# A ring of four PSUM banks that also takes the attention outputs, a new order of work, and identity products on TensorE in the first element

## The chip, the cores and the metric

The kernel runs on one core of one Trainium2 chip. Its engines are called as the profile calls them: PE (matrix products), ACT (activations and copies), DVE (vector work), POOL (small vector work), SP (issues the DMAs). Each engine runs its own queue of instructions in order and waits on semaphores for the others. The metric is the device time of one launch in microseconds. The kernel before took 1795.92 us (median of 3 runs, 1793.83 to 1796.07).

## What is computed

The input x is 32 elements (a batch) of 128 tokens by 256 channels, with a context of the same shape. Four layers follow each other, all in fp32:

```python
x = L0(x, ctx)      # x + attention of element 0 only: one 128x256 block, added to all 32 elements
x = L1(x, ctx)      # RMS norm -> in_proj -> convolution of 4 taps -> silu -> state space scan
                    # -> gate -> RMS norm -> out_proj, residual; then cross attention, 8 heads, padding mask
x = L2(x, ctx)      # causal self attention (16 heads), norm; cross attention, norm; two 256x256 layers, norm
x = L3(x, ctx)      # causal cross attention (16 heads), norm; 256 -> 1024, gelu, 1024 -> 256
```

The scan of L1 is computed in its quadratic form: 128x128 matrices of decays and of pair products (C times B), and then products with the inputs. So an element needs four attentions (numbered 1 to 4 here; attention 0 is L0's and runs once).

## The kernel before, in words

Each of the 32 elements goes through the same 80 or so named tasks: `xhatT` (transpose of the normalised input), `K1`, `V1`, `z0`, `z1`, `xbc0`, `xbc1` (projections), `conv0`, `conv1`, `silu` (DVE and ACT), `pairs` (PE: the pair product `CB`, then a transpose `xh`), `ld` (PE: sums of log decays), `decayed` (DVE), `Y` (PE: the scan's output), `uT`, `proj`, `xnT`, `Q1`, then for each attention `quads` (scores), `scores` (maxima on DVE, exponentials on ACT), `turn` (transposes of the exponentials on PE, copied out by ACT), `values` (products with V), `back` (transpose of the output), `finish` and `norm` (DVE, with a power on POOL in between), and at the end `up0`, `up1`, `down`. On POOL, `dt` and `softplus` are some 20 tiny steps that end in the step sizes, `am` writes the 128x1024 matrix `decay` from them (L1483), and `z0` stands for the gating of z (L1476 and L1477).

The work of several elements is interleaved: while one element is in its last layer, five younger ones are in earlier ones. The order is written out by numbers. `TASKS` gives each task a place in a period of 14 units, element n adds 14 n, `FIRST` and `LAST` shift the tasks of the first eight and last six elements, `SETUP` places what is done once, and `SHIFT` moves a task on ACT, DVE, POOL or SP against its place on PE. Every engine then executes its share of the tasks in the sorted order. Nothing reorders them at run time, so an instruction that waits holds up everything behind it on its engine.

PSUM has eight banks of 128x512 floats. Before, three of them form the ring (`bank[0..2]`), four hold scores, and one is `output`, for `values` alone. A job of the ring is one PE task that fills one bank: job k takes bank k mod 3, in the order of PE's queue. `claim` makes PE wait until job k-3 has been read (semaphore `bank_read`), and the reader, ACT or DVE, waits for `bank_full`. `values` waits for `output_read` instead, and signals by four semaphores `att_full0..3`, one for each 32 rows.

The lines that the text speaks of: L614 transposes (`flip`), L620 and L626 projections, L676 scores, L708 and L718 `values`, L788 `CB`, L795 `ld`, L805 `Y` on PE; L1026 the exponential inside softplus, L992 exponentials of the scores on ACT; L1268 the convolution's steps, L1274 silu's last step, L1282 to L1284 softplus' quotient, L1170 the second half of a norm on DVE.

Of the kernel before, what the change touches and what calls it, by code (L numbers as in the profile page):

```python
# [54 lines left out]
    Q3=37.543, V3=40.148, e3=38.349, n3=39.865, finish3=40.144, norm3=42.354, x4T=42.781, fc1=43.499, fc2=44.959, norm4=44.907,
    K4=45.195, V4=46.057, x5T=46.08, Q4=47.009, finish4=59.44, norm5=59.058, x6T=54.763, up0=56.224, up1=56.439, down=81.976,
    store=80.382, quads1=22.371, scores1_0=22.334, turn1_0=23.905, values1=25.647, quads2=29.409, scores2_0=29.402,
    scores2_1=30.19, turn2_0=31.6, turn2_1=31.809, values2=33.339, attT2=32.223, back2=34.871, quads3=38.411, scores3_0=38.673,
    scores3_1=39.48, turn3_0=40.43, turn3_1=40.496, values3=40.816, attT3=37.17, back3=41.465, quads4=47.824, scores4_0=48.781,
    scores4_1=49.099, turn4_0=50.021, turn4_1=50.308, values4=52.319, attT4=49.603, back4=54.003)  # L60

FIRST = dict(
    loadx=(-1.5564, -2.6165, 0.0017, 3.3707, -0.1049, -5.3785, 0.0062, -0.1984),
    loadc=(-1.6132, 0.0057, 5.0634, 0.2142, -0.0297, -0.0279, 0.0007, -1.9086),
    x1=(-1.6224, 0.0057, -0.0189, -3.0408, -0.0182, -0.03, 0.0203, 0.0012),
    x1r=(-0.0087, -0.0139, 0.0017, -0.0293, 0.0014, 0.001, 0.0251, 0.4294),
    xhat=(0.6085, 0.1762, -0.4078, 0.0017, 0.0014, 0.001, 0.0007, 0.0012),
# [1529 lines left out]
```

## Time and profile before

| | |
|---|---|
| median of 3 runs | 1795.92 us |
| the profiled execution | 1793.13 us, of which the span of instructions 1791.1 us |
| PE busy | 1684.8 us (94% of the span) |
| ACT busy / DVE busy / POOL busy | 1368.2 (76%) / 1345.6 (75%) / 549.9 (31%) |
| mean granted PE clock | 0.978 of full |
| chain that ended last | PE 78%, DVE 14%, ACT 3%, issue 3%, POOL 2% |

Engines are busy side by side, so the shares don't add up. A group of PE rows such as `L620 ... x8` counts passes: an fp32 product of 128 columns is two passes. The time of a group's last pass is modelled and overlaps the next group; the distance from one start to the next is what PE really took. A bracket such as `[0.42 <-DVE conv L1274]` is idle time ahead of the group and who ended it. The loading of the weights fills the DMA engines in the first 50 us; afterwards they move 10 GB/s.

### The profile page before, as it was taken

How to read it: one execution, taken by the hardware profiler on the slowest of the kernel's cores; microseconds unless marked ns; L12 is line 12 of the kernel's file. 1: busy time of each engine (PE TensorE's matmuls, PEld its weight loads, DVE VectorE, ACT ScalarE, POOL GpSimd, SP SyncE). 2: the span in 40 equal slices, each digit the busy share in tenths (PEclk: the TensorE clock that was granted, in tenths of full speed). 3: DMA queues.
4: the chain of work that ended last, by engine and by line, in shares of the span. 5: the costliest groups of instructions: out<-in, count | busy, mean ns of one | idle time of the engine just before them, and what ended most of it. 6: DMA issues, size and time to landing. Idle time of an engine off the chain costs nothing.

```text
span 1791.1 us, 54559 instructions
## 1 busy us (share of the span) xinstructions
PE 1684.8 (94%) x21072; PEld 1437.7 (80%) x21072; DVE 1345.6 (75%) x3355; ACT 1368.2 (76%) x4026; POOL 549.9 (31%) x1288
## 2 busy tenths in 40 slices
PE   5679999999999999999999999999999999999876
PEld 4467888888888888888888888888888888888765
DVE  3477788877777888778788877778888778878542
ACT  2267887887888788788878877887888788778763
POOL 1233233332333333233333333323333233333110
PEclk7799999999999999999999999999999999999988
DMA  7000000000000000000000000000000000000000
GB/s 257 7 7 8 8 2 11 11 11 11 11 2 11 11 11 11 11 11 2 11 11 11 11 11 11 2 11 11 11 11 10 11 2 11 11 8 5 5 4 9
DMA packets 26174, 26.89 MB, mean 15 GB/s; under 512 B 2240, under 2 KB 25024, under 8 KB 25792
## 3 DMA queue, kind: packets, MB, share of 16 engines
q1 hardware_dynamic: 25920, 23.41, 4.0%
q8 instruction: 171, 2.80, 0.7%
q14 instruction: 83, 0.68, 0.1%
HBM read 19.21 MB, written 4.19 MB: 13 GB/s over the span
## 4 chain that ended last, share of the span: by engine, by line
PE 78%; DVE 14%; ACT 3%; issue 3%; POOL 2%; DVEq 0%; DMA 0%; SPq 0%; POOLq 0%; ACTq 0%
PE ring L626 21%; PE ring L620 20%; PE ring L614 17%; PE output L718 5%; PE score L676 5%; DVE conv L1274 4%; PE ring L795 3%; PE ring L805 2%; ACT exps L992 2%; PE output L708 2%; POOL stat L1437 1%; DVE tz L1312 1%; DVE res L1170 1%; DVE bn L1157 1%; DVE res L1358 1%
## 5 line engine op out<-in xcount | busy, mean ns | idle before, releaser
L992 ACT ACTIVATE exps<-score,neg_max 128x128 f32<-128x128 f32 x1808 | 495.0, 412 | 73.3 <-DVE neg_max L1181 70.5
L1181 DVE TENSOR_REDUCE neg_max<-score 128x4 f32<-128x512 f32 x452 | 286.4, 681 | 76.5 <-PE score L676 74.4
L1437 POOL TENSOR_TENSOR stat<-stat 128x1 f32<-128x1 f32 x224 | 129.3, 577 | 530.7 <-DVE stat L1153 529.8
L998 ACT COPY weights<-ring 128x512 f32<-128x512 f32 x452 | 244.0, 604 | 57.2 <-PE ring L614 55.5
L614 PE MATMUL ring<-const,exps 128*128 128x128 f32 x1808 | 248.7, 279 | 24.2 <-ACT exps L992 10.4
L614 PEld LDWEIGHTS ring<-const,exps 128*128 128x128 f32 x1808 | 198.4, 142 | 60.1 <-issue 27.7
L1268 DVE SCALAR_TENSOR_TENSOR conv<-raw,vectors,conv 128x128 f32<-128x128 f32 x576 | 168.4, 348 | 6.8
L620 PE MATMUL ring<-actT,w_q 128*128 128x128 f32 x1024 | 142.5, 282 | 0.5 <-ACT actT L964 0.5
L620 PEld LDWEIGHTS ring<-actT,w_q 128*128 128x128 f32 x1024 | 127.3, 192 | 10.9 <-issue 6.3
L964 ACT COPY actT<-ring 128x256 f32<-128x256 f32 x224 | 81.9, 378 | 70.7 <-PE ring L614 70.6
L676 PE MATMUL score<-K,QB 32*128 32x128 f32 x3616 | 134.9, 283 | 0.1
L676 PEld LDWEIGHTS score<-K,QB 32*128 32x128 f32 x3616 | 113.8, 188 | 16.4 <-issue 15.3
L620 PE MATMUL ring<-actT,w_up 128*128 128x128 f32 x1024 | 123.2, 280 | 0.5 <-ACT actT L964 0.5
L620 PEld LDWEIGHTS ring<-actT,w_up 128*128 128x128 f32 x1024 | 120.5, 197 | 0.9 <-ACT actT L964 0.9
L626 PE MATMUL ring<-w_down,gT 128*128 128x256 f32 x512 | 118.0, 384 | 0.0
L1004 ACT COPY attT<-output 128x512 f32<-128x512 f32 x97 | 56.8, 585 | 75.0 <-PE output L718 75.0
L718 PE MATMUL output<-weights,V 128*32 128x128 f32 x3104 | 106.6, 279 | 2.4 <-issue 1.5
L626 PEld LDWEIGHTS ring<-w_down,gT 128*128 128x128 f32 x512 | 94.9, 190 | 14.8
L620 PE MATMUL ring<-cT,w_k 128*128 128x128 f32 x768 | 104.1, 280 | 0.0
L626 PE MATMUL ring<-w_v,cT 128*128 128x256 f32 x384 | 99.2, 381 | 2.4 <-ACT tz L1040 2.4
L1499 POOL TENSOR_TENSOR V<-V,keep 128x256 f32<-128x256 f32 x64 | 39.7, 621 | 200.2 <-DVE keep L1351 112.1
L620 PEld LDWEIGHTS ring<-cT,w_k 128*128 128x128 f32 x768 | 98.5, 196 | 1.7
(163 smaller groups left out, 3531.2 us busy)
## 6 DMA issues: line engine op xcount, KB each, us to landing
cT<-in_ctxT SPq DMA_DIRECT2D x32, 128.0 KB, 2.2
x_in<-in_x SPq DMA_DIRECT2D x32, 128.0 KB, 2.1
out<-result SPq DMA_DIRECT2D x32, 128.0 KB, 1.7
row_all<-in_rows SPq DMA_DIRECT2D x1, 1420.0 KB, 10.0
w_in<-in_in_proj SPq DMA_DIRECT2D x1, 1288.0 KB, 7.3
w_k<-in_k SPq DMA_DIRECT2D x4, 256.0 KB, 5.8
w_v<-in_v SPq DMA_DIRECT2D x4, 256.0 KB, 5.9
w_q<-in_q SPq DMA_DIRECT2D x4, 256.0 KB, 6.5
```

Source lines behind the costliest of these rows:

```text
L614: last = nc.tensor.transpose(t[:, c * P:(c + 1) * P], src[:, c * P:(c + 1) * P], ident)
L620: last = mm(t[:, at:at + P], w[:, c, cols:cols + P], xT[:, c, :], start=(c == 0), stop=(c == n - 1))
L626: last = mm(t[:, at:at + hi - lo], xT[:, c, :], w[:, c, lo:hi], start=(c == 0), stop=(c == n - 1))
L676: last = mm(score[:, r, at:at + P], QB[rows_of, l, c, e, :], keys[rows_of, l, c, :], start=(not masked and at == 0), stop=(at + P == width))
L718: last = mm(output[ROWS_OF[r], four * P:(four + 1) * P], V2[:, l, h, :], exps_of(t, heads_of(a_, t).index(h)), start=True, stop=True)
L964: nc.scalar.copy(dst.rearrange("p c k -> p (c k)"), t[:, 0:n]).then_inc(read, 1)
L992: last = run(exps[:, n, h * P:(h + 1) * P], of, ACT.Exp, bias=neg_max[:, m, h:h + 1])
L998: nc.scalar.copy(weights[:, buffer(it, a_, l, t, WEIGHT_BUFFERS), half * 4 * P:(half + 1) * 4 * P], t_[:, :]).then_inc(read, 1)
L1181: nc.vector.tensor_reduce(neg_max[:, m, 4 * half:4 * half + 4].rearrange("p (b h) -> p b h", b=each), score[:, first:first + each, 0:4 // ...
L1268: last = stt(conv[:, l % 2, c, :], raw[:, l % 2, c, k:k + P], conv_w[:, c, k:k + 1], conv[:, l % 2, c, :], ALU.mult, ALU.add)
L1274: stt(conv[:, l % 2, :, :], raw[:, l % 2, :, TAPS - 1:], 1.0, conv[:, l % 2, :, :], ALU.add, ALU.mult).then_inc(S["xbc"], 1)
L1437: tt(stat[:, l, 10:11], stat[:, l, 2:3], stat[:, l, 4:5], ALU.pow).then_inc(S[done], 1)
```

## The change

Three things change together.

1. `output` is gone and the ring has four banks. `values1` to `values4` (and `values0`) are jobs of the ring like the others; their readers (`attT` on ACT, `finish1` on DVE) wait for `bank_full` in place of `att_full3` and release `bank_read` in place of `output_read`. What waited for `output_read` on PE (`back`, `Wo`) now waits for the `values` job's bank to be read, unless its own bank makes it wait for the same thing.
2. All tables of the order have new numbers: PE, ACT, DVE, POOL and SP execute the same tasks in another order, in the steady part as in the first and last elements.
3. `SPARE`: ahead of eleven tasks of the first element (one is of the second) PE executes 80 products in all of the 128x128 identity with itself, into the first 128 columns of the bank that the task is about to fill. Nothing reads them.

```diff
 TASKS = dict(
-    loadx=-19.632, loadc=-0.373, x1=-12.582, x1r=18.202, xhat=40.805, xhatT=6.043, dt=11.125, softplus=10.471, am=-3.466,
...
+    loadx=-39.297, loadc=-21.957, x1=-31.388, x1r=0.609, xhat=34.036, xhatT=-8.817, dt=1.27, softplus=-2.884, am=-12.308,
...
-RING_BANKS = 3
+RING_BANKS = 4
...
+SPARE = {("turn0_0", 0): 5, ("turn0_1", 0): 4, ("bias", 0): 7, ("xhatT", 0): 17, ("pairs", 0): 18, ("Y", 0): 5, ("uT", 0): 4,
+         ("turn1_0", 0): 5, ("Wo", 0): 6, ("Y", 1): 4, ("x4T", 0): 5}
...
-NO_RING += [f"{task}{a_}" for task in ("quads", "values", "attT") for a_ in PARTS]
+NO_RING += [f"{task}{a_}" for task in ("quads", "attT") for a_ in PARTS]
...
-        output = pb("output", [P, 512])
...
+            def spare(it, what, lane, times):
+
+                t, full = claim(it, what, lane)
+                for _ in range(times):
+                    mm(t[:, 0:P], ident, ident, start=True, stop=True)
...
             def values(it, a_, l):
 
-                if a_:
-                    pe.wait_ge(S["output_read"], nth_output(it, a_, l) - 1)
+                output, full = claim(it, f"values{a_}", l)
...
-                            last.then_inc(S[f"att_full{r}"], 1)
+                            last.then_inc(full if r == TILES - 1 else S[f"att_full{r}"], 1)
 
             def back(it, a_, l):
-                pe.wait_ge(S["output_read"], nth_output(it, a_, l))
+                evacuated(it, f"values{a_}", l, back_job(a_, l))
...
             def program():
                 for task, l, i in ORDER["PE"]:
+                    if i == 0 and (task, l) in SPARE:
+                        spare(Of(i), RING_JOBS.get(task, task).split()[0], l, SPARE[task, l])
                     if task in do:
...
             def out_turned(it, a_, l):
-                for r in range(TILES):
+                for r in range(TILES - 1):
                     act.wait_ge(S[f"att_full{r}"], nth_output(it, a_, l))
-                nc.scalar.copy(attT[:, att_buffer(it, a_, l), :], output[:, :]).then_inc(S["output_read"], 1)
+                t, read = filled(it, f"values{a_}", l)
+                nc.scalar.copy(attT[:, att_buffer(it, a_, l), :], t[:, :]).then_inc(read, 1)
...
                 def finish1(l):
-                    for r in range(TILES):
+                    for r in range(TILES - 1):
                         dve.wait_ge(S[f"att_full{r}"], nth_output(it, 1, l))
-                    step(nc.vector.reciprocal(rec1[:, :], output[:, D:]))
+                    t, read = filled(it, "values1", l)
+                    step(nc.vector.reciprocal(rec1[:, :], t[:, D:]))
```

**PE, the first element.** From the transpose of attention 0's output (`attT`) to the sums of log decays (`decay,const`). Before:

```order
L614 MATMUL ring0<-const,attT 128x128 x4
L614 MATMUL ring1<-const,att 128x128 x2
L620 MATMUL ring2<-cT,w_k1 128x128 x4
L626 MATMUL ring0<-w_in,actT 128x264 x2
L620 MATMUL ring1<-actT,w_in 128x128 x6
L620 MATMUL ring2<-actT,w_in 128x128 x6
L626 MATMUL ring0<-w_v1,cT 128x256 x2
L626 MATMUL ring1<-w_in,actT 128x256 x2
L788 MATMUL ring2<-conv 128x128
L614 MATMUL ring0<-const,conv 128x128 x4
L795 MATMUL ring1<-decay,const 128x512
L795 MATMUL ring2<-decay,const 128x512
```

In the changed kernel (`ring3<-const 128x128 x17` are identity products):

```order
L569 MATMUL ring2<-const,attT 128x128 x4
L576 MATMUL ring3<-const 128x128 x17
L569 MATMUL ring3<-const,att 128x128 x2
L581 MATMUL ring0<-cT,w_k1 128x128 x4
L581 MATMUL ring1<-actT,w_in 128x128 x6
L581 MATMUL ring2<-actT,w_in 128x128 x6
L587 MATMUL ring3<-w_in,actT 128x264 x2
L587 MATMUL ring0<-w_v1,cT 128x256 x2
L587 MATMUL ring1<-w_in,actT 128x256 x2
L576 MATMUL ring2<-const 128x128 x18
L748 MATMUL ring2<-conv 128x128
L569 MATMUL ring3<-const,conv 128x128 x4
```

The two halves of `xbc` (`actT,w_in ... x6`) now come ahead of `z1` (`w_in,actT 128x264`), and 17 and 18 identity products stand ahead of `xhatT` and of the pair product of `conv`.

**POOL, the middle of the program**, around `am` (`decay<-const,dts`) and the gating of z (`tz<-tz`, `zs<-tz,zs`). Before:

```order
L1490 TENSOR_TENSOR q_first<-QB,const 128x16
L1482 TENSOR_TENSOR dts<-dts,row_all 128x8
L1483 TENSOR_TENSOR decay<-const,dts 128x1024
L1509 TENSOR_TENSOR fc1T<-res,row_all 128x256
L1476 TENSOR_SCALAR tz<-tz 128x512
L1477 TENSOR_TENSOR zs<-tz,zs 128x512
```

And now:

```order
L1445 TENSOR_TENSOR dts<-dts,row_all 128x8
L1446 TENSOR_TENSOR decay<-const,dts 128x1024
L1462 TENSOR_TENSOR V<-V,keep 128x16x16
L1464 COPY V<-keep 128x16
L1400 TENSOR_TENSOR stat<-stat 128x1
L1472 TENSOR_TENSOR fc1T<-res,row_all 128x256
L1400 TENSOR_TENSOR stat<-stat 128x1
L1453 TENSOR_TENSOR q_first<-QB,const 128x16
L1439 TENSOR_SCALAR tz<-tz 128x512
L1440 TENSOR_TENSOR zs<-tz,zs 128x512
```

`decay` was written right ahead of the gating of z. It now comes ahead of a masking of V (`V<-V,keep`) and of two powers (`stat<-stat`), and right ahead of the gating stand only a power and `q_first`.

**DVE, the middle of the program**, around silu's last step (`conv<-raw,conv`). Before:

```order
L1358 SCALAR_TENSOR_TENSOR res<-att,mask,res 128x256
L1157 BN_STATS bn<-res 128x6
L1158 BN_AGGR stat<-bn 128x2
L1153 TENSOR_SCALAR stat<-stat 128x1
L1168 SCALAR_TENSOR_TENSOR att<-res,stat,row_all 128x256
L1170 SCALAR_TENSOR_TENSOR res<-att,stat,row_all 128x256
L1274 SCALAR_TENSOR_TENSOR conv<-raw,conv 128x768
L1347 TENSOR_SCALAR nonzero<-ring 128x16
L1181 TENSOR_REDUCE neg_max<-score 128x4 x2
```

And now:

```order
L1321 SCALAR_TENSOR_TENSOR res<-att,mask,res 128x256
L1120 BN_STATS bn<-res 128x6
L1121 BN_AGGR stat<-bn 128x2
L1116 TENSOR_SCALAR stat<-stat 128x1
L1164 TENSOR_TENSOR res<-x_in,att 128x256
L1131 SCALAR_TENSOR_TENSOR att<-res,stat,row_all 128x256
L1133 SCALAR_TENSOR_TENSOR res<-att,stat,row_all 128x256
L1116 TENSOR_SCALAR stat<-stat 128x1
L1310 TENSOR_SCALAR nonzero<-ring 128x16
L1237 SCALAR_TENSOR_TENSOR conv<-raw,conv 128x768
L1144 TENSOR_REDUCE neg_max<-score 128x4 x2
```

Silu's last step now comes after `x1` (`res<-x_in,att`), its mean square (the last `stat<-stat`) and `e2` (`nonzero<-ring`), which stood behind it.

## Rows read from the trace of the kernel before

**Rows 1.** Busy us of each engine (x instructions) by stretch, clock, DMA share, GB/s.
```profile
30.40:66.20 35.80, 20.23 (x135) 15.15 (x135) 15.57 (x44) 7.21 (x19) 11.95 (x28) 0.69 0.14 47
...
92.90:139.40 46.50, 36.54 (x472) 29.57 (x472) 34.22 (x85) 28.29 (x85) 16.22 (x37) 0.95 0.02 7
...
919.10:1648.00 728.90, 717.77 (x9171) 616.43 (x9171) 585.02 (x1457) 593.45 (x1751) 240.20 (x561) 1.00 0.03 9
...
1740.00:1791.10 51.10, 35.50 (x249) 29.47 (x247) 12.28 (x30) 17.73 (x50) 3.40 (x6) 0.81 0.03 8
```

**Rows 2.** PE in time order: start, us, line, op, tiles; idle before and releaser.
```profile
919.07 0.49 PE L788 MATMUL ring<-conv 128*128 128x128 f32 x2 [0.42 <-DVE conv L1274]
...
920.73 2.15 PE L795 MATMUL ring<-decay,const 128*128 128x512 f32 x4
922.71 1.03 PE L626 MATMUL ring<-w_fc,fc1T 128*128 128x256 f32 x4
```

**Rows 3.** The same view of PE, 14 elements later.
```profile
1647.98 0.49 PE L788 MATMUL ring<-conv 128*128 128x128 f32 x2 [0.42 <-DVE conv L1274]
```

**Rows 4.** Waits of PE from 200 to 1600 us: total, times, longest.
```profile
PE ring L788 <- DVE conv L1274: 11.0, 26, 0.4
```

**Rows 5.** POOL and DVE in time order where the element 17 pair product waits.
```profile
916.25 1.95 POOL L1483 TENSOR_TENSOR decay<-const,dts 128x1024 f32<-128x1024 f32 x1
916.37 2.65 DVE L1274 SCALAR_TENSOR_TENSOR conv<-raw,conv 128x768 f32<-128x768 f32 x1
...
919.57 1.51 POOL L1476 TENSOR_SCALAR tz<-tz 128x512 f32<-128x512 f32 x1
```

**Rows 6.** The same for element 3, from 184 us.
```profile
188.71 0.95 DVE L1274 SCALAR_TENSOR_TENSOR conv<-raw,conv 128x768 f32<-128x768 f32 x1
...
188.93 2.49 POOL L1483 TENSOR_TENSOR decay<-const,dts 128x1024 f32<-128x1024 f32 x1
...
190.92 0.49 PE L788 MATMUL ring<-conv 128*128 128x128 f32 x2
```

**Rows 7.** L1274 alone: ns at least, median and most.
```profile
L1274 DVE SCALAR_TENSOR_TENSOR conv<-raw,conv x32: 950/2646/2648, 45.7 to 1645.3; 128x768 f32<-128x768 f32 x32
```

**Rows 8.** PE in time order, the first element.
```profile
30.43 0.69 PE L614 MATMUL ring<-const,att 128*128 128x128 f32 x2 [3.85 <-DVE att L1209]
...
46.68 0.79 PE L788 MATMUL ring<-conv 128*128 128x128 f32 x2 [7.08 <-DVE conv L1274]
...
49.70 3.50 PE L795 MATMUL ring<-decay,const 128*128 128x512 f32 x4 [1.37 <-POOL decay L1483]
...
60.03 3.44 PE L626 MATMUL ring<-w_out,tz 128*128 128x256 f32 x8 [0.72 <-issue]
...
66.17 0.48 PE L614 MATMUL ring<-const,att 128*128 128x128 f32 x2 [2.48 <-DVE att L1163]
...
92.89 0.49 PE L788 MATMUL ring<-conv 128*128 128x128 f32 x2 [1.08 <-DVE conv L1274]
```

**Rows 9.** PE in time order, 125 to 200 us.
```profile
135.81 0.69 PE L614 MATMUL ring<-const,res 128*128 128x128 f32 x2 [3.65 <-DVE res L1170]
...
142.04 1.88 PE L795 MATMUL ring<-decay,const 128*128 128x512 f32 x4
143.76 1.03 PE L626 MATMUL ring<-w_fc,fc1T 128*128 128x256 f32 x4
...
152.43 1.89 PE L626 MATMUL ring<-w_out,tz 128*128 128x256 f32 x8
```

**Rows 10.** ACT in time order, the first element's exponential of its step sizes.
```profile
39.05 0.20 ACT L1026 ACTIVATE dts<-dts 128x8 f32<-128x8 f32 x1
```

**Rows 11.** PE in time order, the last element.
```profile
1754.25 3.62 PE L626 MATMUL ring<-w_down,gT 128*128 128x256 f32 x16
...
1766.92 1.93 PE L718 MATMUL output<-weights,V 128*32 128x128 f32 x32 [0.83 <-issue]
...
1775.49 5.93 PE L620 MATMUL ring<-actT,w_up 128*128 128x128 f32 x32 [0.46 <-ACT actT L964]
```

More of the change, by code:

```diff
@@ L55 @@
[L55 to L58, printed above, removed]
@@ new lines @@
+    loadx=-39.297, loadc=-21.957, x1=-31.388, x1r=0.609, xhat=34.036, xhatT=-8.817, dt=1.27, softplus=-2.884, am=-12.308,
+    xbc0=-7.003, xbc1=-5.859, z1=-5.461, z0=1.147, K1=-7.656, V1=-0.645, conv0=10.153, conv1=1.914, silu=8.942, pairs=2.154,
+    ld=3.18, decayed=4.453, Y=4.486, uT=5.016, proj=5.731, xnT=7.896, Q1=8.272, finish1=10.278, Wo=13.01, x2T=13.36, K2=15.065,
+    Q2=13.819, V2=18.506, e2=15.211, n2=15.74, finish2=23.561, norm2=19.381, x3T=23.838, row=23.91, K3=24.14, Q3=25.27, V3=24.234,
@@ new lines @@
+    e3=26.002, n3=26.41, finish3=21.372, norm3=36.468, x4T=29.166, fc1=31.148, fc2=31.994, norm4=36.026, K4=31.657, V4=32.925,
+    x5T=32.94, Q4=33.558, finish4=46.075, norm5=40.873, x6T=41.8, up0=42.154, up1=42.297, down=68.294, store=78.752, quads1=9.708,
+    scores1_0=10.704, turn1_0=11.473, values1=12.06, quads2=15.325, scores2_0=16.842, scores2_1=17.864, turn2_0=18.34,
+    turn2_1=18.516, values2=19.823, attT2=22.328, back2=21.152, quads3=25.921, scores3_0=25.992, scores3_1=26.33, turn3_0=26.863,
@@ L602, in evacuated, with evacuated_all @@
                     pe.wait_ge(bank_read[b], use + 1)
-            def evacuated_all(it, *jobs):
+            def evacuated_all(it, *jobs, then=None):
                 last = {job(it, *j)[0]: j for j in sorted(jobs, key=lambda j: place(it, *j))}
                 for j in last.values():
-                    evacuated(it, *j)
+                    evacuated(it, *j, then)
             def flip(it, what, lane, src, n):
@@ L699, in exps_of @@
                     return weights[:, buffer(it, a_, l, t, WEIGHT_BUFFERS), i * P:(i + 1) * P]
-                evacuated_all(it, *V_job, *[j for t in range(PARTS[a_]) for j in turn_jobs(a_, l, t)])
+                evacuated_all(it, *V_job, *[j for t in range(PARTS[a_]) for j in turn_jobs(a_, l, t)], then=(f"values{a_}", l))
                 if a_ == 1:
@@ L720, in values @@
                         if four == H16 // TILES - 1:
[L721 removed]
+                            last.then_inc(full if r == TILES - 1 else S[f"att_full{r}"], 1)
             def back(it, a_, l):
[L724 removed]
+                evacuated(it, f"values{a_}", l, back_job(a_, l))
                 flip(it, *back_job(a_, l), attT[:, att_buffer(it, a_, l), :], 4)
@@ L828, in Wo @@
             def Wo(it, l):
-                pe.wait_ge(S["output_read"], nth_output(it, 1, l))
+                evacuated(it, "values1", l, ("Wo", l))
                 project(it, "Wo", l, square["o1"], actT[:, l])
```

245 lines of the change are left out of this document (96 added, 149 removed).

## The prediction

> **What bounds the kernel now.** First the busy time by stretch [rows 1]: from 919 to 1648 us, which is 14 elements, PE is busy 717.77 of 728.9 us, so the middle of the program is PE's and the other engines can only hurt by making it wait. In the first element (30 to 66 us) PE is busy 20.2 of 35.8 us at a granted clock of 0.69, from 93 to 139 us it idles 10 of 46.5 us, and in the last 51 us it idles 15.6. I then looked for the period: `CB` of an element starts at 919.07 and 14 elements later at 1647.98 [rows 2, 3], so an element costs 728.91 / 14 = 52.06 us.
>
> How much of that is work? Eight fp32 products of 128 columns take from 142.04 to 143.76, 0.215 us each [rows 9]. Adding up the start-to-start times of all of an element's PE tasks where nothing waits gives me 50.7 us. So 1.36 us of each period are lost: 0.80 as visible idle time (11.13 / 14, rows 1), the rest inside groups. The idle time has one large author: `CB` waits 0.42 us for silu's last step on DVE, 26 times between 200 and 1600 us [rows 4]. Inside a group, `ld` takes from 920.73 to 922.71, 1.98 us, where 1.72 do [rows 2, 9], for its halves need banks that others still read. What is left, some 0.6 us, are hand-overs of 0.2 to 0.3 us in which a transpose or a `turn` claims one of three banks or waits for a norm.
>
> Why silu is late is in the DVE rows: L1274 takes 0.95 us at least and 2.65 as a rule [rows 7]. In the rule it starts 0.12 us after POOL began to write `decay`, and ends 0.82 us after POOL is done [rows 5]: it did nothing until POOL had finished. In element 3 silu started 0.22 us ahead; it took 0.95, POOL took 2.49, and `CB` did not wait [rows 6]. Whoever is first makes the other wait.
>
> **Part 1, the ring.** 58 jobs an element on three banks become 62 on four. Measured in PE work between the end of a bank's last job and its next claim, by my count along both orders, the shortest distances were 0.49 us (`Q4` after `x5T`) and a dozen of 0.88; now they are 0.94 (`turn3`'s second half after `down`), 1.32, and then 1.6 to 1.8. A copy of a bank takes 0.4 to 0.6 us and starts 0.2 after PE, so distances of 0.88 are where the hand-overs bite. The new risk is that `values1` holds a ring bank through DVE's reciprocal: the bank is wanted by `turn3` four jobs later, 4.0 us of PE work on, and I count 3.4 us until `finish1` is done. No instruction is added outside SPARE. Value: between 0 and the 0.6 us of hand-overs; I take 0.35 an element, since the norm waits among them only shrink.
>
> **Part 2, the middle's order.** `decay` leaves silu's neighbourhood on POOL, which removes 1.7 us from DVE's path to `CB`. What is late next? I followed the ACT queue from `up0`: gelus, tanh, gelus, the copy of `K2`, the square of `x1`, then z0's two copies, which release the gating (1.5 us on POOL, rows 5). Silu stands behind `x1`'s mean square and `e2`. By durations of the trace silu starts some 0.3 us ahead of the gating and ends 0.1 to 0.2 us after PE reaches `CB`. So of the 0.42 I keep 0.2. With `pairs` no longer pushed, `ld` loses its 0.26 (its claims now lie 1.6 us and more from the last use). Further `x2T` and `x4T` stood 0 to 0.9 us of work behind the products they depend on and now have 1.8 and 5.3 us. In sum 0.35 (ring) + 0.22 (`CB`) + 0.25 (`ld`) = 0.8 us an element, bounds 0 and 1.2, over the 29 elements from the third on: 23 us (0 to 35).
>
> **Part 3, the start.** Three things. (a) The clock. `ld` takes 3.50 us in element 0 and 1.88 later, `proj` 3.44 and 1.89 [rows 8, 9]: half rate. Each came behind idle time. At the full rate the pieces on the first element's chain (outputs' product, transposes, projections of `z` and `xbc`, `ld`, `uT`, `proj`) are some 7 us shorter. (b) The order. The two `xbc` now directly follow `K1`, so the convolution begins 1.8 us earlier in PE work; the exponential of the step sizes, at 39.05 us behind V1 in ACT's queue [rows 10], now comes right after `z1`, so that POOL's chain to `decay` can start some 3 us earlier; and ahead of `xnT` PE executes `K1` and half of `xbc` of element 1 (2.2 us), where it idled 2.48 us at 66.17 [rows 8]. Together with (a) I get `xnT` at about 58 us, with 2.2 us more work done: 10 us gained. In element 1, `conv0` moves ahead of `finish1`, and `CB`, at 92.89 us after a wait of 1.08 [rows 8], comes at about 79. (c) From there to `CB` of element 2 the largest idle time is 3.65 us before `x4T` [rows 9], of which `K2` and `z0` (1.8 us), now in between, take half; but other waits of this stretch [rows 1] stay. I carry 15 us for the start as a whole and 2 for the ramp behind it.
>
> The price are 80 products. At 0.215 us they are 17 us, at half rate 34. The waits they stand in were 3.85 us before `xhatT` and 7.08 before `CB` [rows 8]; 17 and 18 products at the full rate fill 3.7 and 3.9 of them. `CB`'s wait shrinks by the work under (b) to about 6 us, so 18 fit at full rate and not at half rate. The seven before `bias` (1.5 us) push `back` by some 0.8 us, but `values` ahead of them is 0.9 shorter if the clock is up. So at the full rate I price SPARE at nothing, at half rate up to 17 us minus the remaining slack, some 8.
>
> **Part 4, the end.** `down` of element 29 stood between `Q4` and `quads4` of the last element, where ACT needs 1.8 us to copy `Q4` [rows 11]. It now stands between `values4` and `back4`, where only 0.9 us are covered: `quads4` starts 1.8 us earlier and `back4` 2.7 later than it could. `values4` and `up0` ran at a lower rate there (1.93 and 5.93 us, rows 11), and `down` may too. I take 1 us lost, bounds -3 and +4.
>
> **The sum**, against the profiled execution: 1791.1 - 23 - 15 - 2 + 1 = 1752 us of span, and 2.0 us around it, 1754. The median stands 2.8 us above that execution (1795.92 to 1793.13), so the forecast is 1757 us.
>
> **Rivals.** (A) The start as forecast, the middle unchanged: the 1.36 us are then set by DVE and ACT (80 to 81% busy each, rows 1), and a wait removed at `CB` returns a task later, as the 0.72 us of idle time in front of other tasks would. For it: both have only 10 us of 52 to spare, and their queues are as rigid as PE's. Against it: half of PE's idle time has one author [rows 4], and its cause is seen. 1796 - 16 = 1780 us.
>
> (B) The identity products cost what they bring: the granted clock doesn't stay up between them, and they are served at half rate, 34 us, half of it outside the waits. The start gains 5 instead of 17: 1769 us.
>
> (C), the slower side: the gating of z wins against silu. Then silu waits the whole L1476 (1.5 us) and takes its 0.95 afterwards, and `CB` waits some 2.0 us in each element in place of 0.42. It decides from the point where z0's copies end less than about 0.25 us after `e2`'s read; my margin is 0.3. The middle then loses 1.6 and keeps the other 0.6 of gain: 29 x 1.0 = 29 us slower, the start 16 faster: 1796 + 13 = 1809 us.
>
> In a sentence of the Trainium skill (SBUF — State Buffer, "Who interferes with whom"): a DVE instruction with two SBUF inputs contends with a GpSimd instruction that reads SBUF, through an exclusive lock held for the whole instruction. The trace agrees (2.65 and 0.95 us, rows 5 to 7). The page speaks for both the gain of part 2 and rival C, as the gating reads SBUF too; by it the price of C is a whole L1476.
>
> **How the numbers follow.** Forecast 0.60, A 0.14, B 0.12, C 0.10, and 0.04 for something that I don't see, half of it slower. The forecast's own range is 1742 to 1772; A adds the part up to 1782, and with B below it 0.8 is held by 1740 to 1785. This kernel's runs lie within 0.13%, so 0.2% tells a change. Faster: forecast, A, B and half of the rest, 0.88, less 0.04 in which A and B are both true and next to nothing is left, which is the same; slower: C and half of the rest, 0.12.
>
> **What would show it.** In the profile after: L1274 at a median near 0.95 us and `CB` waiting under 0.2 us (part 2), or L1274 at 2.4 and `CB` waiting 2 us (C). Starts of `CB` 51.2 us apart in the middle (forecast), 52 (A). `ld` of element 0 at about 1.9 us and the clock of 30 to 60 us above 0.9 (a), or below 0.8 with the identity products at 0.43 us each (B). `CB` of element 1 near 79 us. In the last 51 us, `back4` 2 to 3 us after `values4`. Wrong altogether would be a period longer than 52.1 us with L1274 short: then a new wait has taken the place of the old ones.

## The result and the profile after

The changed kernel takes 1737.63 us (median of 4 runs, 1736.11 to 1740.05), the kernel before 1795.41 in the same runs: a ratio of 0.968, interval 0.966 to 0.970. The forecast was 1757 us with 1740 as the low end. The sign was right, the size was not: the change gains 57.8 us where 39 were forecast. The span of the profiled execution fell from 1791.1 to 1734.3 us, by 56.8. One execution of each of two kernels below (5762 us of i1, its profiled one, and 3523 us of i3) was disturbed and is left out of their times, so i1 has no row in the table.

First the stretches that answer to [rows 1], in the same columns (length; busy us of PE, of its weight loads, of DVE, ACT and POOL; clock, DMA share, GB/s):

```profile
30.00:66.00 36.00, 27.43 (x221) 23.40 (x222) 16.35 (x47) 8.36 (x23) 12.81 (x29) 0.86 0.15 52
88.80:132.00 43.20, 37.66 (x494) 31.57 (x491) 31.64 (x83) 28.02 (x84) 15.05 (x37) 0.98 0.02 5
891.70:1598.70 707.00, 704.59 (x9170) 611.37 (x9171) 570.31 (x1454) 588.09 (x1748) 230.72 (x561) 1.00 0.03 9
1683.20:1734.30 51.10, 35.45 (x272) 29.28 (x260) 12.20 (x32) 19.82 (x53) 3.43 (x6) 0.87 0.03 9
```

The third row is the middle, the same 14 elements and 9170 products as before. PE idles 2.4 us there where it idled 11.1. But its busy time fell as well, from 717.77 to 704.59 us for the same work: the larger part of the gain (13.2 of 21.9 us) never was idle time.

PE in time order, middle of the program (start, us, line, tiles, count, idle before and its releaser), answers to [rows 2, 3]:

```profile
891.73 0.49 PE L748 MATMUL ring<-conv 128*128 128x128 f32 x2 [0.19 <-DVE conv L1237]
...
893.38 1.88 PE L755 MATMUL ring<-decay,const 128*128 128x512 f32 x4
895.11 1.05 PE L581 MATMUL ring<-cT,w_k 128*128 128x128 f32 x8
...
942.26 0.49 PE L748 MATMUL ring<-conv 128*128 128x128 f32 x2 [0.19 <-DVE conv L1237]
```

In this element `CB` waits 0.19 us instead of 0.42, as forecast (0.2), and `ld` takes from 893.38 to 895.11, 1.73 us instead of 1.98, as forecast. `CB` starts 14 elements after 891.73 at 1598.71: 706.98 / 14 = 50.50 us an element. That is below the 50.7 us that the prediction took for pure work.

The waits of PE from 200 to 1600 us (total, times, longest), where [rows 4] had 11.0 us in its first row:

```profile
PE ring L748 <- DVE conv L1237: 4.1, 21, 0.2
PE ring L569 <- ACT attT L967: 1.7, 1, 1.7
PE ring L569 <- DVE res L1133: 1.5, 2, 1.3
```

Silu against the gating of z, POOL and DVE in time order, answers to [rows 5]:

```profile
890.25 1.51 POOL L1439 TENSOR_SCALAR tz<-tz 128x512 f32<-128x512 f32 x1 [1.43 <-ACT tz L1003]
890.32 1.36 DVE L1237 SCALAR_TENSOR_TENSOR conv<-raw,conv 128x768 f32<-128x768 f32 x1
```

And silu's line alone, all 32 (ns at least, median and most), answers to [rows 7]:

```profile
L1237 DVE SCALAR_TENSOR_TENSOR conv<-raw,conv x32: 947/1351/1365, 46.0 to 1597.6; 128x768 f32<-128x768 f32 x32
```

The gating starts 0.07 us ahead of silu: the condition of rival C has come true. But silu then takes 1.36 us, not 1.5 + 0.95. It loses 0.41, and is not held until POOL has ended at 891.76: it ends at 891.68.

The first element, PE in time order, answers to [rows 8]:

```profile
31.96 0.44 PE L569 MATMUL ring<-const,att 128*128 128x128 f32 x2 [2.04 <-DVE att L1172]
...
40.05 4.18 PE L576 MATMUL ring<-const 128*128 128x128 f32 x36
47.03 0.80 PE L748 MATMUL ring<-conv 128*128 128x128 f32 x2 [2.79 <-DVE conv L1237]
49.77 3.73 PE L755 MATMUL ring<-decay,const 128*128 128x512 f32 x4 [1.09 <-POOL decay L1446]
...
64.60 0.44 PE L569 MATMUL ring<-const,att 128*128 128x128 f32 x2 [0.47 <-DVE att L1126]
```

`CB` of element 0 comes at 47.03 us (46.68 before), `xnT` at 64.60 where 58 were forecast, `CB` of element 1 at 88.83 where 79 were. The 18 identity products ahead of `CB` run at nearly the full rate (36 passes in 4.18 us, 0.23 us a product). But 2.79 us of idle time are left behind them, and `ld` is served at half rate again: 3.73 us. The clock from 30 to 60 us is 0.83, where the forecast asked for above 0.9 and rival B for below 0.8.

The last element, answers to [rows 11]:

```profile
1709.92 1.08 PE L678 MATMUL ring<-weights,V 128*32 128x128 f32 x32 [0.96 <-ACT weights L960]
1710.93 3.72 PE L587 MATMUL ring<-w_down,gT 128*128 128x256 f32 x16
...
1718.61 0.44 PE L569 MATMUL ring<-const,res 128*128 128x128 f32 x2 [3.52 <-DVE res L1133]
1719.51 5.21 PE L581 MATMUL ring<-actT,w_up 128*128 128x128 f32 x32 [0.46 <-ACT actT L926]
```

From `values4` to the end it is 24.4 us (24.2 before). `back4` (not shown, at 1714.49 us) starts 4.6 us after `values4` and not 2 to 3. The end gained, but ahead of this row.

**Where the 56.8 us are.** The starts of `CB` cut the span of any of these kernels in three: up to `CB` of element 2, the 29 elements to `CB` of element 31, and what lies behind. This table has every version whose trace could be read so; ratios are against the kernel before in the same runs, with their 95% intervals. The last three columns come from one profiled execution each, which is not always a typical one: that of g1 took 5.2 us more than g1's median, that of f4 2.9 us less.

| version | us | ratio | CB of 2 | per element | behind CB of 31 |
|---|---|---|---|---|---|
| before | 1795.4 | | 139.4 | 52.02 | 143.1 |
| after | 1737.6 | 0.968 (.966-.970) | 132.0 | 50.58 | 135.6 |
| f1 ring of four alone | 1771.4 | 0.987 (.986-.989) | 144.1 | 51.23 | 142.0 |
| f2 new order, three banks | 1827.0 | 1.018 (1.016-1.019) | 136.6 | 53.39 | 140.5 |
| f3 after without SPARE | 1739.8 | 0.969 (.968-.971) | 135.9 | 50.57 | 136.1 |
| f4 before with SPARE | 1790.2 | 0.997 (.996-.999) | 133.4 | 52.07 | 142.0 |
| g1 `decay` back at the gating | 1740.1 | 0.970 (.969-.971) | 132.2 | 50.74 | 139.7 |
| g2 silu first | 1731.9 | 0.965 (.964-.966) | 130.8 | 50.41 | 136.2 |
| g3 earlier preparation | 1737.9 | 0.968 (.967-.969) | 131.7 | 50.65 | 135.7 |
| g4 `down` back | 1737.0 | 0.968 (.966-.969) | 131.3 | 50.60 | 136.7 |
| h1 before, `decay` early | 1818.9 | 1.014 (1.012-1.015) | 143.8 | 52.77 | 141.7 |
| h2 f1, `decay` early | 1792.4 | 0.999 (.998-1.000) | 143.2 | 52.03 | 141.3 |
| h3 g2 and g3 | 1733.0 | 0.966 (.964-.967) | 132.0 | 50.46 | 138.2 |
| h4 f1 with three banks | 1926.9 | 1.073 (1.071-1.075) | 144.6 | 56.74 | 143.1 |
| i2 g2, products at the end | 1731.2 | 0.965 (.963-.966) | 131.2 | 50.46 | 136.8 |
| i3 h3, products at both ends | 1729.6 | 0.964 (.962-.965) | 127.1 | 50.44 | 135.5 |
| i4 after, V1 moved back | 1780.3 | 0.992 (.991-.993) | 134.5 | 52.01 | 136.4 |

So the start gives 7.4 us, the middle 29 x 1.445 = 41.9, the end 7.5. The prediction had 17, 23 and -1.

### The profile page after: what moved, and what is told of

It is laid out like the page before. It is cut to its first block, busy times and chain, and to the rows that moved or that the text cites. A ratio compares the mean times of both kernels' runs of the same rounds, so it can differ in the third digit from the quotient of the medians.

```text
span 1734.3 us, 54906 instructions
## 1 busy us (share of the span) xinstructions
PE 1664.1 (96%) x21232; PEld 1438.0 (83%) x21232; DVE 1313.4 (76%) x3355; ACT 1357.1 (78%) x4026; POOL 533.5 (31%) x1288
## 4 chain that ended last, share of the span: by engine, by line
PE 88%; DVE 7%; issue 2%; ACT 1%; POOL 1%; DMA 0%; DVEq 0%; SPq 0%; POOLq 0%; ACTq 0%
PE ring L581 26%; PE ring L587 22%; PE ring L569 18%; PE score L637 6%; PE ring L678 5%; PE ring L755 3%; PE ring L765 2%; DVE conv L1237 2%; PE ring L668 2%; PE ring L816 1%; DVE conv L1231 1%; PE score L628 1%; DVE neg_max L1144 1%; PE ring L748 1%; ACT exps L954 1%
## 5 line engine op out<-in xcount | busy, mean ns | idle before, releaser
L960 ACT COPY weights<-ring 128x512 f32<-128x512 f32 x452 | 257.3, 658 | 44.0 <-PE ring L569 42.3
L569 PE MATMUL ring<-const,exps 128*128 128x128 f32 x1808 | 240.1, 275 | 11.6 <-ACT exps L954 7.9
L569 PEld LDWEIGHTS ring<-const,exps 128*128 128x128 f32 x1808 | 210.2, 142 | 33.9 <-ACT exps L954 15.8
L581 PE MATMUL ring<-actT,w_q 128*128 128x128 f32 x1024 | 138.0, 278 | 2.5 <-ACT actT L926 2.5
L637 PEld LDWEIGHTS score<-K,QB 32*128 32x128 f32 x3616 | 113.8, 188 | 21.9 <-issue 21.7
L926 ACT COPY actT<-ring 128x256 f32<-128x256 f32 x224 | 86.4, 386 | 56.3 <-PE ring L569 56.3
L678 PE MATMUL ring<-weights,V 128*32 128x128 f32 x3104 | 104.9, 276 | 4.1 <-issue 2.1
L967 ACT COPY attT<-ring 128x512 f32<-128x512 f32 x97 | 57.0, 588 | 63.9 <-PE ring L678 63.3
L678 PEld LDWEIGHTS ring<-weights,V 128*32 128x32 f32 x3104 | 79.0, 109 | 25.7 <-issue 25.5
```

Of the source, the lines that this page charges most:

```text
L569: last = nc.tensor.transpose(t[:, c * P:(c + 1) * P], src[:, c * P:(c + 1) * P], ident)
L581: last = mm(t[:, at:at + P], w[:, c, cols:cols + P], xT[:, c, :], start=(c == 0), stop=(c == n - 1))
L637: last = mm(score[:, r, at:at + P], QB[rows_of, l, c, e, :], keys[rows_of, l, c, :], start=(not masked and at == 0), stop=(at + P == width))
L678: last = mm(output[ROWS_OF[r], four * P:(four + 1) * P], V2[:, l, h, :], exps_of(t, heads_of(a_, t).index(h)), start=True, stop=True)
L926: nc.scalar.copy(dst.rearrange("p c k -> p (c k)"), t[:, 0:n]).then_inc(read, 1)
L960: nc.scalar.copy(weights[:, buffer(it, a_, l, t, WEIGHT_BUFFERS), half * 4 * P:(half + 1) * 4 * P], t_[:, :]).then_inc(read, 1)
```

## The experiments

**f1 and f2: the two halves of the change.** f1 has the code after (four banks, the outputs of attention in them) with the tables of numbers before and no identity products. f2 is the reverse: the code before with the tables after.

```
f1:  RING_BANKS = 4      TASKS, FIRST, LAST, SETUP, SHIFT: before   SPARE = {}
f2:  RING_BANKS = 3, output in its own bank                         tables: after
```

> The ring of four banks with the outputs in it, in the order of before, without identity products. Theory R (the fourth bank carries the middle of the program): the period falls from 52.0 to about 51 us and the time to about 1765 us. Theory O (the order carries it): CB still waits 0.42 us and L1274 still takes 2.65 us, only hand-overs of banks get shorter, 0.3 us an element: about 1786 us.

> The new order with the three banks and the separate output bank of before, without identity products. Theory O: the period is 50.9 us or less and the time about 1755 us, nearly all of the gain of the middle. Theory R, and a theory B by which each needs the other: the new order was made for four banks, with three its shortest distances are short again, the period stays at 51.5 us or more and the time at 1775 us or more.

The ring alone takes 0.80 us off an element. The order alone makes it 1.37 us longer, but on four banks it takes another 0.65 off. The gain is not a sum of two: the new order is written for four banks. The waits of PE in f2 show what three banks do to it; all the releasers are copies and reads that empty a bank:

```profile
PE ring L572 <- DVE keep L1303: 20.5, 26, 0.8
PE ring L578 <- ACT weights L950: 12.5, 26, 0.5
PE ring L572 <- ACT raw L983: 11.1, 26, 0.8
PE ring L572 <- ACT V L933: 9.4, 26, 0.7
PE ring L566 <- DVE result L1341: 7.1, 25, 0.3
```

In f1 `CB` still waits its 0.42 us, 26 times, but `ld` falls to 1.74 and the wait of a `turn` on `tz` is gone but for one:

```profile
912.17 0.49 PE L795 MATMUL ring<-conv 128*128 128x128 f32 x2 [0.42 <-DVE conv L1284]
...
913.83 1.88 PE L802 MATMUL ring<-decay,const 128*128 128x512 f32 x4
915.57 1.13 PE L634 MATMUL ring<-w_fc,fc1T 128*128 128x256 f32 x4
```

So the ring alone gives `ld`'s 0.25 us, which the prediction booked to the order. The order alone gives it as well: in f2, with three banks, `ld` starts at 942.54 and the next group at 944.26 us (1.72). Either half is enough, and the 0.25 must not be counted twice.

**h4: is it the fourth bank, or the outputs in the ring?** f1 with one number changed, so that the outputs of attention share three banks.

```
-RING_BANKS = 4
+RING_BANKS = 3
```

> The code of the changed kernel in the order of before, without identity products, with a ring of three banks that also takes the outputs: the bank that was freed is left unused. Theory R2 (what gives the 24 us of the ring alone is the fourth bank): 62 jobs then share three banks, values has to wait for banks and holds them through its readers, and the time is 1805 us or more. Rival (what gives it is that the outputs rotate, so that values no longer waits for output_read): 1790 us or less.

```profile
PE ring L634 <- DVE keep L1361: 63.9, 23, 3.7
PE ring L795 <- DVE conv L1284: 10.1, 24, 0.4
```

An element takes 4.7 us more than before, 5.5 more than with four. A job waits up to 3.7 us for a bank that DVE is to read. Part of the 5.5 us is the clock, which falls with these waits: over the 14 elements behind `CB` of element 17 it is granted 0.96 in h4 and 1.00 in f1, and PE is busy 748.2 us there against 709.8. Sharing costs; the bank pays for it and for 0.8 us more.

**g1 and g2: silu against POOL.** g1 puts `decay` back beside the gating on POOL. g2 puts silu earlier into DVE's queue, ahead of `x1r` and `e2`.

```
g1:  FIRST am=(0, 0, ...)           SHIFT POOL am=10.06185 -> 15.59
g2:  SHIFT DVE silu=-6.49255 -> -6.84255
```

> The changed kernel with one task moved on POOL: the writing of decay (am) again right ahead of the gating of z, as before the change. Theory L (what made silu late before was POOL reading SBUF at the same time, and the 128x1024 write of decay costs it 1.7 us, while the gating costs it 0.4): L1237 goes from 1.36 back to 2.6 us or more, CB waits 1.2 us or more, the period goes from 50.5 to 51.5 to 52.5 and the time to 1765 to 1795 us. Rival (the moves on DVE and ACT ended the wait, POOL's place is of no weight): L1237 stays under 1.4 and the time within 2 us.

> The changed kernel with silu's last step moved ahead of x1's mean square and e2 on DVE, some 0.9 us earlier than the gating of z on POOL. Theory L: it takes 0.95 us in place of 1.36, CB no longer waits 0.19 us, the period falls from 50.53 to 50.2 to 50.35, the time to 1728 to 1733 us. Rival (0.2 us come back at the next task of PE): period and time stay within 2 us of the changed kernel.

POOL and DVE of g1 in time order:

```profile
894.58 1.96 POOL L1446 TENSOR_TENSOR decay<-const,dts 128x1024 f32<-128x1024 f32 x1
...
895.88 1.47 DVE L1237 SCALAR_TENSOR_TENSOR conv<-raw,conv 128x768 f32<-128x768 f32 x1
```

Silu starts 1.30 us into the write of `decay`, ends 0.81 us after it, and `CB` waits 0.31. Yet from element 17 to 31 an element takes 50.45 us, after's 50.50. DVE gets back elsewhere more than it loses at silu (1.47 against 1.36 us): its step `res<-att,res` (L1319), which runs into the write of `decay` in the order after (0.67 us at the median, 200 to 1600 us), takes 0.42 in g1. g1's profiled execution is longer where its clock was lower: 5.5 us from `CB` of element 2 to that of 17 (0.993 against 0.998) and 4.1 behind the last `CB` (0.889 against 0.924). The medians differ by 2.4 us and the intervals of the ratios overlap. So `decay`'s place beside the gating is not what the order gains by, and the expected cost did not show. DVE and POOL of g2:

```profile
886.05 0.95 DVE L1237 SCALAR_TENSOR_TENSOR conv<-raw,conv 128x768 f32<-128x768 f32 x1
...
887.17 1.51 POOL L1439 TENSOR_SCALAR tz<-tz 128x512 f32<-128x512 f32 x1 [1.43 <-ACT tz L1003]
```

Silu is done before the gating begins, takes 0.95 us, and `CB` waits in no element but the first: another 0.17 us an element, 1731.9 us in all. Here the rest of `CB`'s wait (0.19) is worth what it was.

**h1 and h2: `decay` moved early, with nothing else.** In the kernel before (h1) and in f1 (h2) `decay` is written right behind the step sizes, as in the new order.

```
h1, h2:  SHIFT POOL am=16.54316 -> 14.4761; FIRST and LAST of am: those of softplus
```

> The kernel before with one task moved: on POOL the writing of decay directly follows the step sizes, some 10 us ahead of silu's last step, as in the changed kernel. Theory L (silu is late in it only because it waits for this write): L1274 takes 0.95 us, CB doesn't wait 0.42 us, the period falls from 52.02 to 51.4 to 51.6 us and the time by 12 to 18 us, to about 1780. Rival (with three banks the next hand-over takes the time): CB's wait goes, the time falls by under 5 us.

> The ring of four banks in the order of before, without identity products (1771.4 us, period 51.25), with the same one move on POOL. Theory L: CB no longer waits, the period falls to about 50.8 and the time to 1756 to 1760 us; what then still separates it from the changed kernel without identity products (1739.8 us) is the rest of the new order. Rival: the wait returns elsewhere and the time stays above 1766 us.

The theory that silu's lock was the order's gain falls here. In the middle `CB` waits no more in either, and both are slower than without the move, by 0.75 us an element (h1) and 0.80 (h2). The waits of PE in h1 say where:

```profile
PE ring L614 <- DVE res L1170: 17.0, 27, 0.9
PE ring L614 <- DVE res L1337: 13.3, 25, 1.5
```

The 0.42 us at `CB` have become 0.6 and 0.5 us in front of two transposes of a residual. DVE and POOL of h1 in time order say why:

```profile
920.50 1.90 POOL L1483 TENSOR_TENSOR decay<-const,dts 128x1024 f32<-128x1024 f32 x1
921.68 0.99 DVE L1356 TENSOR_TENSOR res<-att,res 128x256 f32<-128x256 f32 x1
...
931.98 1.05 DVE L1170 SCALAR_TENSOR_TENSOR res<-att,stat,row_all 128x256 f32<-128x256 f32 x1 [0.51 <-POOL stat L1437]
932.04 0.72 POOL L1509 TENSOR_TENSOR fc1T<-res,row_all 128x256 f32<-128x256 f32 x1
```

The write of `decay` left silu and met another DVE step, L1356, which takes 0.99 us at the median here and in h2 and 0.42 in the kernel before and in f1. POOL's `fc1T`, which stood behind `decay`, moved up and met a norm, L1170: it takes over 0.9 us once an element in h1 and h2, and once in all from 200 to 1600 us in the kernel before. Both DVE steps end 0.27 us after POOL's, and each delays one of the two transposes. It looks like rival A's "a wait removed at `CB` returns a task later", but what returns is the same interference at two other steps. In the order after, the first of these steps takes 0.67 us and no norm is lengthened (L1133: 0.49 us at most from 200 to 1600 us).

**i4: how much is distance in PE's queue worth?** One number of the new table: V1, a product of 0.87 us that stands between `Wo` and `x2T`, goes back behind `K3`.

```
-V1=-0.645
+V1=-3.83
```

> The changed kernel with one number of the table changed: V1 goes back to where the kernel before had it, between K3 and V3 of the other stage, so that it no longer stands between the output projection and x2T; the PE work between them falls from 1.78 to 0.89 us. Theory distance: a hand-over of 0.89 us costs 0.2 to 0.3 us each time, 5 to 10 us in all: 1742 to 1748 us, with a new wait of L569 on DVE's res (L1133) in each element. Rival: distance does not matter as long as silu is in time; within 2 us of 1737.6.

It costs 42.7 us, 1.46 an element: as much as the whole change gained in the middle. Four to nine times what was expected. The waits of PE:

```profile
PE ring L569 <- ACT V L943: 9.6, 26, 0.4
PE ring L569 <- DVE res L1133: 6.9, 26, 0.4
PE ring L569 <- DVE res L1300: 5.8, 22, 0.3
PE ring L678 <- issue: 5.5, 26, 0.5
```

The second and third are one thing. DVE's timeline of the kernel after begins this stretch with the reciprocal of attention 1 and ends it with the norm that `xhatT` waits for:

```profile
925.30 1.75 DVE L1295 RECIPROCAL rec<-ring 128x256 f32<-128x256 f32 x1
...
939.27 0.48 DVE L1133 SCALAR_TENSOR_TENSOR res<-att,stat,row_all 128x256 f32<-128x256 f32 x1
939.92 0.15 DVE L1116 TENSOR_SCALAR stat<-stat 128x1 f32<-128x1 f32 x1 [0.17 <-ACT att L971]
```

Between these rows DVE has no idle time: 14.4 us of queue from 925.30 on. In i4 it is the same (950.30 to 964.85). Over these 15 us DVE's queue is at least as long as PE's work, though PE is 99.7% busy over the middle as a whole. The reading that fits is that V1's 0.87 us of PE work filled the difference: taken out, they come back as waits at `x2T` (L1300) and `xhatT` (L1133), and are to be done elsewhere too. A part of it is again POOL: in i4 the step `res<-att,res` (L1319) takes 0.87 us at the median, 0.67 in the kernel after. There V1 also stands ahead of V3 in ACT's queue, whose copy is late for a `turn` that claims its bank (0.37 us). The run changes two things, then: the distance, and the neighbourhood of V3; 9.6 of the 27.8 us of waits are the second, and the 5.5 us of the last row are neither. It shows that a place in the order can be worth as much as the whole change, not that V1's is the only such place.

**What a wait costs beside its idle time.** PE of i4 in time order:

```profile
943.09 1.06 PE L581 MATMUL ring<-actT,w_q 128*128 128x128 f32 x8
944.51 1.10 PE L569 MATMUL ring<-const,exps 128*128 128x128 f32 x8 [0.37 <-ACT V L943]
```

From start to start, `Q` to `turn`, it is 1.42 us, where the same product with no wait behind it takes 0.89. The wait of 0.37 costs 0.53. In the kernel before a `turn` at 926.45 is followed by the next at 927.77 after a wait of 0.22; 1.32 us where 0.87 do: it costs 0.45.

```profile
926.45 1.09 PE L614 MATMUL ring<-const,exps 128*128 128x128 f32 x8
927.77 1.07 PE L614 MATMUL ring<-const,exps 128*128 128x128 f32 x8 [0.22 <-DVE tz L1312]
```

Taking for each group of an element the shortest start-to-start time of the same group in five of these traces, the kernel before has 3.6 us over this sum (period 51.98), f1 2.8 (51.17), after 2.4 (50.53), i4 3.8 (51.96) and g2 2.1 (50.30). Less the visible idle time (0.80 and 0.17 us an element) that leaves 2.8 and 2.2, so stalls inside groups account for some 0.6 of the 0.94 us an element by which PE's busy time fell. Start to start and without the visible idle time, the `turn` products of an element take 6.96 us before, 6.39 in f1 and 6.44 after, `ld` 1.99, 1.76 and 1.73, and `up0` with `up1` 3.79, 3.79 and 3.57. The rows count as busy what a group loses when its successor stalls; whether they also hide late weights was not looked at.

**f3, f4, g3: the start.** f3 is after without identity products, f4 before with them, g3 after with three preparations set earlier in DVE's queue.

```
f3:  SPARE = {}
f4:  before + SPARE, spare() and its call in program()
g3:  prep_in=-125.2505 -> -127.05, prep_masks=-123.7236 -> -126.9, prep_out=-123.6283 -> -126.8
```

> The changed kernel without its 80 identity products. If they keep the clock up in the first two elements, the time rises from 1737.6 by 3 to 8 us and the granted clock from 20 to 60 us falls from 0.83 to about 0.65. If they cost what they bring, it is 1737.6 within 2 us.

> The kernel before with the 80 identity products at the same places and nothing else. If they are worth something by themselves: 3 to 7 us faster than before, CB of the first element up to 2 us earlier. If they fit only the new order, same or up to 5 us slower, since its waits are elsewhere.

> The changed kernel with the preparations (rates on ACT, scaling of weights and masks on DVE) in their place of before, ahead of the end of attention 0. My explanation of why the start gave 7 and not 15 us: these steps stand in DVE's queue in front of x1, xhatT of the first element comes at 31.96 us behind 2.0 us of idle time, and that drops the clock for the xbc projections. Then xhatT comes at about 30, its wait vanishes, xbc takes 2.7 in place of 4.1 us, CB of the first element comes 2 to 3.5 us earlier and the time falls by as much. Rival (the chain through dt on POOL sets the first element's pace in any case): the time falls by under 1.5 us.

The products gain 6.0 us up to `CB` of element 2 in the old order and 3.9 in the new (5.6 and 2.2 in the medians, the 2.2 with overlapping intervals of the ratios); the new order without them gains 3.4, and both together 7.4. The clock from 20 to 60 us is 0.87 with them in the kernel after and 0.63 without (f3), a larger step than the time shows. An earlier chain alone is no gain: in g3 `CB` of element 0 comes 2.8 us earlier (44.23), and at element 2 nothing of it is left (131.65 against 132.0). PE behind it:

```profile
44.23 0.49 PE L748 MATMUL ring<-conv 128*128 128x128 f32 x2 [2.68 <-DVE conv L1237]
46.96 3.78 PE L755 MATMUL ring<-decay,const 128*128 128x512 f32 x4 [1.72 <-POOL decay L1446]
```

Two idle stretches, then `ld` at half rate. The granted clock of g3's stretch from 86 to 132 us is 0.89, after's 0.96.

**h3, i1, i3: products where the clock still fell.** h3 is g2 and g3 together. i1 is h3 with 29 instead of 18 products ahead of `CB`, 7 ahead of `ld` and 5 ahead of `turn3_1`. i3 is i1 with the products of i2 (below).

```
+ ("pairs", 0): 29, ("ld", 0): 7, ("turn3_1", 0): 5
```

> The changed kernel with both silu's last step moved ahead (1731.9 us alone) and the preparations in their place of before (no gain alone: 2.8 us earlier at CB of the first element, given back in the second by a fall of the granted clock at 117 us). If that fall is a matter of phase, the gain of the start may stay this time: 1729 to 1731 us. If it returns whenever the first elements are early, 1732 to 1734 us.

> The changed kernel with silu ahead of x1r and e2 and the earlier preps on DVE (as in h3_silu_and_start, 1732.96 us), and more identity products in the first element: 29 instead of 18 ahead of CB, 7 more ahead of ld, 5 more ahead of turn3_1 of the first element. Theory clock: the start's missing gain is PE at the lower rate behind idle windows; then ld of element 0 takes 1.9 instead of 3.8 us, the row at 117 us full rate, CB of element 2 comes some 3 us earlier than h3's 132.0, and the time is 1729 to 1730 us. Rival chain: the first element is set by POOL and DVE; CB of element 2 within 1 us of 132.0, time within 1 us of 1733. Rival cost: the products are served at half rate and push CB; 1735 or more.

> i1 and i2 together. If both theories of the clock hold the gains add: 1726 to 1728 us. If neither: 1733 to 1737.

h3 adds nothing to g2 (1733.0 against 1731.9). i1's median is 1732.7 us (1730.59 to 1732.77). i3 has the same start and a readable trace:

```profile
36.39 6.64 PE L578 MATMUL ring<-const 128*128 128x128 f32 x58
42.86 0.39 PE L750 MATMUL ring<-conv 128*128 128x128 f32 x2
...
46.11 1.98 PE L757 MATMUL ring<-decay,const 128*128 128x512 f32 x4 [0.85 <-POOL decay L1450]
```

`ld` takes 1.98 us instead of 3.8, the clock from 30 to 80 us is 1.00, and `CB` of element 2 comes at 127.1 us, 4.9 earlier than in h3. The theory of the clock is right for what it says of these rows. In the medians it is small: i3 is 3.3 us below h3 but only 2.3 below g2, and the intervals of the two ratios overlap (0.9624 to 0.9649, 0.9636 to 0.9663). i1's median does not show its share. i3 is the fastest version here, 1729.6 us, 8.0 below the changed kernel.

**g4 and i2: the end.** g4 puts `down` of element 29 back between `Q4` and `quads4`. i2 is g2 with 35 identity products in the waits of the last element.

```
g4:  LAST down=(0.0411, -0.0673, -0.2268, 0, 0, 0) -> (..., -6.62, 0, 0)
i2:  SPARE_LAST = {"turn4_0": 8, "values4": 3, "x6T": 15, "x5T": 9}
```

> The changed kernel with down of element 29 back between Q4 and quads4 of the last element. My step said that the new place costs about 1 us: then the time falls by 0 to 2 us. Rival (a full PE there keeps the clock up and ACT's table load is what counts): it rises by 1 to 3 us.

> g2_silu_first (1731.91 us) with identity products in the last element alone: 8 ahead of turn4_0, 3 ahead of values4, 15 ahead of x6T, 9 ahead of x5T. Theory clock: w_up of the last element takes 3.7 instead of 5.2 us and down less than 7; the part of the span behind the last CB falls from 136.2 to 133.5 to 134.7 us, time 1729 to 1730.5. Rival: the clock there does not follow such products; they only push the chain, 1732 to 1735 us.

Moving `down` changes nothing (1737.0 against 1737.6). In i2 `up0` and `up1` of the last element take 3.84 us instead of 5.42, as expected, but `values4` now comes 1.2 us later behind `CB` of element 31 (112.8 against 111.6), and nothing is left (1731.2 against 1731.9).

## Why the prediction was wrong

**The floor.** "50.7 us of work" was the step that failed first. It came from rows in which nothing waits visibly. Such rows still hold stalls, as the fall of the busy time shows. With 1.36 us as all there was to gain, 0.8 looked bold; 1.45 came, and g2 runs at 50.31.

**Part 1 and 2, the middle: 23 us forecast, 41.9 measured.** This is the step that put the forecast out of its range. The terms at `CB` (0.22) and `ld` (0.25) came as forecast, 0.23 and 0.25. The mis-sized term is the ring's 0.35 "of the 0.6 us of hand-overs". By f1 the ring with `ld` gives 0.80 (0.60 forecast), so 0.55 without it. The order on top gives 0.65, of which `CB` explains 0.23; the rest, 0.42, had no price in the prediction at all. It noted that `x2T` and `x4T` "now have 1.8 and 5.3 us" and let it go. Of the 0.42, 0.22 lies in `up0` and `up1`, which stand ahead of `xhatT` (3.79 us in f1, 3.57 after). That distance to the norms gives it is the reading that i4 supports, with its two changes in one; it was not tested alone. h1 and h2 show the other half of the order's work: the two POOL writes must not meet a DVE step on which a transpose waits. Rival A's "0.72 us of idle time in front of other tasks" was a slip: 0.80 [rows 1] less the 0.42 at `CB` is 0.38.

**Rival C** had the right condition and the wrong price. The margin of 0.3 us was not there (-0.07). The price of 2.0 us a `CB` was taken from a lock held for the whole instruction. With the write of `decay` the rows do look so: a start 0.12 us late costs 1.70 us [rows 5]. With the gating of 512 columns silu loses 0.41 us. The Trainium skill (SBUF — State Buffer, "Who interferes with whom") names a lock held for the whole instruction: this trace agrees for `decay` and not for the gating, and the measurement decides. What tells the two apart was not tested alone. The gating has one tensor as its input, `decay` two. Width does not decide: in h1 `fc1T`, only 256 columns wide but with two tensors as inputs, holds a DVE step as `decay` does.

**Rival A** did not come true in the new order. In h1 and h2 the wait did return a task later, but not because the queues of DVE and ACT are full: DVE's steps were lengthened by POOL.

**Part 3, the start: 17 us forecast, 7.4 measured.** (a) The clock was half right. The 18 identity products ahead of `CB` run at nearly the full rate, as priced (the six ahead of `Wo` do not: 12 passes in 2.61 us), but the stretch from 40 to 50 us is granted 0.82, and `ld`, forecast at 1.9, takes 3.73 behind 2.8 and 1.1 us of idle time. i3 has the full clock and gains 4.9 us over h3, not 7. (b) failed: "POOL's chain to `decay` can start some 3 us earlier". DVE does its preparations ahead of the norm that `xhatT` waits for, so `xhatT` itself comes 1.5 us later than before (31.96), and `decay` begins at 47.82 (47.75 before). From there on the whole first element was booked 6 to 7 us too early. That SPARE costs nothing in sum was right.

**Part 4, the end: -1 forecast, +7.5 measured.** The move of `down` was priced at 1 us lost, and g4 shows 0. The gain is elsewhere. Behind `CB` of element 31 come another 93 us in which the pipeline of stages drains, and only then the last `fc2`. `up0` of the element before last comes 5.2 us earlier behind that `CB` (86.2 us, 91.5 before), the last `fc2` 6.6 us (93.3 and 100.0), and the rest of the way takes 42.3 us instead of 43.1. The prediction treated as "the end" only the last 51 us. The clock has a share in it: behind that `CB` it is granted 0.893 before and 0.924 after, and in f1 and f2, with 142.0 and 140.5 us, 0.890 and 0.901. Which change of the order brings the rest was not tested.

**Luck.** The start brought 9.6 us less than forecast and the end 8.5 us more. They nearly cancel, so the miss of the sum (57.8 us gained, 38.9 forecast) is as large as that of the middle alone, and hides two others half as large.

The risk that `values1` holds a ring bank through the reciprocal is seen once in after, 1.22 us at 119.76 us, and in no steady element.

## What to carry to other kernels

A bound computed over a long stretch hides local ones: follow each queue from one row with idle time to the next, and where another engine's queue runs without a gap for many microseconds, try work of the main engine there. In i4 a product of 0.87 us taken away from such a place cost 1.46 us an element. Do not take rows without a visible wait for a floor: compare start-to-start times of the same group in several places first. Before moving an instruction that delays a wait you know, look what runs beside its new place, and beside the place of whatever moves up behind it: in h1 and h2 the delay came back there. And read the granted clock of a stretch before comparing it between two executions.

## What the runs showed of the hardware that was not expected

A wait of PE costs more than its idle time: 0.53 us for 0.37 and 0.45 for 0.22 (rows above), and 0.49 for 0.42 at `CB` (the scores' group ahead of it takes 1.59 us from start to start in the kernel before and 1.10 where nothing follows late). A DVE step with two SBUF inputs beside a POOL instruction lost 1.70 us against one writing 128x1024 from two tensors, 0.57 against one writing 128x256 from two, and 0.41 against one of 128x512 from one. PE came to the lower clock in the kernel after in or behind idle times of 2.04, 2.79 and 3.23 us, but at 74 us also behind 0.86, 0.38 and 0.77 us shortly after each other. In i3 it stayed at the higher one from 30 us on with idle times of 0.4 to 1.0 us, the same three among them, and came to the lower one at 80 us, behind 3.11. So the length of the last idle time alone does not tell.
